# Splitting 1092 product columns at 512 and 1024 instead of 364 and 728 in an fp32r matmul kernel

## The chip, the cores and the metric

One core of a Trainium2 chip runs the kernel. The metric is the device time of one execution in microseconds (us), lower is better. Before the change it is 508.02 us, the median of two runs (507.74 and 508.31).

## The reference

A batch of 64 matrices x of 64 x 1024 is mixed along its 64 channels with weights that depend on a condition, then goes through a feed-forward layer with a low-rank branch whose rank is chosen row by row, and is added to x.

```python
# condition: two small gelu layers, softmax over K = 8 kernels
att   = softmax(gelu(gelu(cond @ W0 + b0) @ W1 + b1) @ W2 + b2)      # (64, 8)
agg_w = einsum('bk,koi->boi', att, weight);  agg_b = att @ bias_k      # (64, 64, 64), (64, 64)
h     = einsum('boi,bih->boh', agg_w, x) + agg_b[:, :, None]           # (64, 64, 1024)
# feed-forward: W is 1024 x 1024, A is 64 x 1024, gate_w is 4 x 1024
scores = h @ gate_w.T + gate_b                                         # 4 ranks: 8, 16, 32, 64
sel    = argmax(scores)                                                # top-1, its weight is 1
out    = x + h @ W.T + b + (h @ A[:r].T) @ B[:, :r].T                  # r = rank selected per row
```

## The kernel before

The 64 x 64 rows of x are taken as T = 32 tiles of 128 rows (two batch elements each). The channel mixing is moved behind the big product: for each tile the kernel first computes z = x [W | A | gate], with 1024 + 64 + 4 = 1092 columns (`NCOL`), and then multiplies z from the left by the block-diagonal mixing weights `bd`. The last 68 columns are u, from which the rank is selected and the low-rank branch computed.

Every fp32 operand is split into a high and a low part (`xth`, `xtl`; `wh`, `wl`; `zh`, `zl`; `bd` with two parts), both of type fp32r, and a product is made of three passes: high x high, low x high, high x low. The contraction of z runs over 1024 inputs in `KC` = 8 chunks k of 128. So z takes 8 x 3 matmuls for each group of columns; the stationary operand is a 128x128 block of `xth` or `xtl`, another one for each matmul, and the moving operand is a row of columns of `wh` or `wl`.

The 1092 columns are cut into `BANKS` = 3 groups of `CB` = 364 (cut by `bank_columns`, L239), each into a PSUM bank of 512 fp32. Group 2 (columns 728 to 1091) holds 296 columns of W and the 68 of u. A tile works on its groups in the `ORDER` (2, 0, 1); m is the place in that order. z of a group goes to one of two PSUM banks `p_z` in turn (`ring`); the mixed result goes to `p_out`, three banks for each of two tiles.

What each engine does for tile j, in its program's order (the kernel is written by hand with semaphores; PE executes in program order):
- PE (`step` L716, `main` L629, `mix` L640, `lora` L664): m = 0: 24 matmuls, after k = 3 `mix(j-1, 2)`, after k = 5 `lora(j-1)`; m = 1: 24 matmuls, after k = 3 `mix(j, 0)`; m = 2: 24 matmuls, after k = 3 `mix(j, 1)`, after k = 4 the transpose of u (L662). A mix is 3 matmuls (L653, L654, L657) and waits for `zl` of its group (L645). lora is 2 matmuls (L670, L671) for each of the three groups: 296 columns in group 2, 364 in the others.
- ACT: `z_hi` (L385) copies z to `zh` when the last pass of the group is done; also `xth` (L370), `bd` (L377), the transposed u (L393). In tile 1 it also copies the column sums (L436).
- DVE: `z_lo` (L480) makes `zl` = z - `zh`; then `xtl` (L457), the mixing weights (L463, L466), `residual` (L490, L493: the sum of `p_out` and `xin` into `ysum`, which shares memory with `wraw`), `route` (L514 to L535: the choice of the rank).
- POOL makes the bias terms (L322 to L337). SP issues all loads and stores.

So `mix(j-1, 2)`, which stands behind the first 12 matmuls of tile j, needs z_hi and z_lo of the group that was finished as the last of tile j-1. Tile 0 is written apart (L685 to L712): it loops over k outside and the three groups inside, as W arrives. The last tile ends with `lora` per group, `mix` (L759 to L763), `last_residual` (L496) and three stores.

Of the kernel before, what the change touches and what calls it, by code (L numbers as in the profile page):

```python
# [5 lines left out]
F32 = mybir.dt.float32  # L6
F32R = mybir.dt.float32r
ALU = mybir.AluOpType
# [24 lines left out]
def adaln_ffn(nc, x, xt, layer0, layer12, b2, kernels, bias_k, wag, b, bt, gate_b, out):  # L33
# [10 lines left out]
    RE = R + E  # L44
    NCOL = O + RE
    BANKS = 3
    CB = NCOL // BANKS
    UNROLL = 4
    ROW_BH, ROW_BL = 64, 96
    FIRST = 2  # L50
    ORDER = (2, 0, 1)
    assert P == 2 * C and HID == P and NB == C and UNROLL % 2 == 0
    assert layer0.shape[1] == NB + HID + 1 and layer12.shape[1] == HID + K + 1 and wag.shape[1] == NCOL
    assert NCOL % (2 * BANKS) == 0 and CB <= BANK and O > (BANKS - 1) * CB
    assert len(RANKS) == E and RANKS[-1] == R == C and T % UNROLL == 0 and T * K <= BANK // 2 and 2 * T <= P

    x_t = x.rearrange("(t b) c h -> t (b c) h", b=2)
# [2 lines left out]
    with ExitStack() as ctx:  # L60
# [14 lines left out]
        wl = sb("wl", [P, KC, NCOL], F32R)  # L75
        bt_h = sb("bt_h", [P, O], F32R)
        bt_l = sb("bt_l", [P, O], F32R)
        zh = sb("zh", [P, 2, CB], F32R)
        zl = sb("zl", [P, 2, CB], F32R)
        ident = sb("ident", [P, P])  # L80

        wsum = sb("wsum", [P, NCOL])
# [146 lines left out]
        def z_place(i, j, m):  # L229

            if not follows(i, j, 1) and m > 0:
                return p_out[:, 1, m - 1, 0:CB]
            return p_z[:, ring(j, m), 0:CB]

        def u_place(i, j):

# [1 line left out]

        def bank_columns(n):  # L239

            return slice(n * CB, min((n + 1) * CB, O))

        @block.sync
        def _(sp):
            sp.dma_start(cw0[:, :], layer0).then_inc(s_cond0_in, 16)
            sp.dma_start(xtin[:, 0, 0:FIRST * P], xt[0][:, 0:FIRST * P]).then_inc(s_xt_first_in, 16)
            for k in range(KC):
                sp.dma_start(wraw[:, k, :], wag[k * P:(k + 1) * P, :]).then_inc(s_w_in[k], 16)
                if k == 0:
                    sp.dma_start(xtin[:, 0, FIRST * P:], xt[0][:, FIRST * P:]).then_inc(s_xt_in[0], 16)  # L250
                    sp.dma_start(b2r[:, :], b2.partition_broadcast(NB)).then_inc(s_cond2_in, 16)
                    sp.dma_start(bk[:, :], bias_k).then_inc(s_bk_in, 16)
            sp.dma_start(xtin[:, 1, :], xt[1]).then_inc(s_xt_in[1], 16)
            for h in (slice(0, C), slice(C, P)):
                sp.dma_start(kern[h, :, :], kernels).then_inc(s_kern_in, 16)
            sp.wait_ge(s_clear, 2)
            sp.dma_start(gbias[:, R:RE], gate_b.partition_broadcast(P)).then_inc(s_gate_in, 16)
            for r in (ROW_BH, ROW_BL):
                sp.dma_start(brow[r:r + 1, :], b.rearrange("(a o) -> a o", a=1)).then_inc(s_lora_in, 16)
            for h in (slice(0, R), slice(R, P)):  # L260
                sp.dma_start(bt_raw[h, :], bt).then_inc(s_lora_in, 16)
            sp.dma_start(xin[:, 0, :], x_t[0]).then_inc(s_x_in[0], 16)
            for t in range(1, UNROLL):
                if t >= 2:
                    sp.dma_start(xtin[:, t, :], xt[t]).then_inc(s_xt_in[t], 16)
                sp.dma_start(xin[:, t, :], x_t[t]).then_inc(s_x_in[t], 16)

            def store(i, j):
                sp.wait_ge(s_y, i * UNROLL + (j + 1))
                sp.dma_start(out_t[i * UNROLL + j], ysum[:, j % 2, :]).then_inc(s_stored[j % 2], 16)  # L270

            with sp.Fori(0, T // UNROLL - 1) as i:
                for j in range(UNROLL):
                    sp.wait_ge(s_xtl, i * UNROLL + (j + 1))
                    sp.dma_start(xtin[:, j, :], xt[i * UNROLL + (j + UNROLL)]).then_inc(s_xt_in[j], 16)
                    store(i, j)
                    sp.dma_start(xin[:, j, :], x_t[i * UNROLL + (j + UNROLL)]).then_inc(s_x_in[j], 16)
            for j in range(UNROLL - 1):
                store(T // UNROLL - 1, j)
            for m, n in enumerate(ORDER):  # L280
                cols = bank_columns(n)
                sp.wait_ge(s_y, T + m)
                sp.dma_start(out_t[T - 1][:, cols], ysum[:, (T - 1) % 2, cols]).then_inc(s_stored[(T - 1) % 2], 16)
            sp.wait_ge(s_stored[0], 16 * T // 2)
            sp.wait_ge(s_stored[1], 16 * (T // 2 + BANKS - 1))

        @block.gpsimd
        def _(pool):
# [67 lines left out]
        def _(act):  # L356
# [23 lines left out]
            def z_hi(i, j, m):  # L380

                act.wait_ge(s_z, banks_before(i, j, m + 1))
                if follows(i, j, 1) or m >= 2:
                    act.wait_ge(s_mix, banks_before(i, j, m - 1))
                nc.scalar.activation(zh[:, ring(j, m), :], z_place(i, j, m), ACT.Copy).then_inc(s_zh, 1)  # L385

            def u_transposed(i, j):

# [37 lines left out]
            def step(i, j):  # L426
                if follows(i, j, 2):
                    z_hi(i, j - 1, 2)
                    if precedes(i, j):
                        xt_hi(i, j + 1)  # L430
                        bd_hi(i, j + 1)
                z_hi(i, j, 0)
                if not follows(i, j, 2):

                    act.wait_ge(s_colsum_mm, 1)
                    nc.scalar.activation(colsum[:, :].rearrange("p (a n) -> p a n", n=CB), p_out[:, 1, :, 0:CB],  # L436
                                         ACT.Copy).then_inc(s_colsum, 1)
                    bd_hi(i, j + 1)
                z_hi(i, j, 1)
                if not follows(i, j, 2):  # L440
                    u_transposed(i, j - 1)
                u_transposed(i, j)
# [5 lines left out]
        def _(dve):  # L448
# [27 lines left out]
            def z_lo(i, j, m):  # L476

                dve.wait_ge(s_zh, banks_before(i, j, m + 1))
                at = ring(j, m)
                nc.vector.tensor_tensor(zl[:, at, :], z_place(i, j, m), zh[:, at, :].bitcast(F32),  # L480
                                        ALU.subtract).then_inc(s_zl, 1)

            def residual(i, j):
# [2 lines left out]
                dve.wait_ge(s_xb, i * UNROLL + (j + 1))  # L486
                if follows(i, j, 2):
                    dve.wait_ge(s_stored[j % 2], i * 16 * (UNROLL // 2) + 16 * (j // 2))
                full = (BANKS - 1) * CB
                nc.vector.tensor_tensor(ysum[:, j % 2, 0:full].rearrange("p (a n) -> p a n", n=CB),  # L490
                                        p_out[:, j % 2, 0:BANKS - 1, 0:CB],
                                        xin[:, j % UNROLL, 0:full].rearrange("p (a n) -> p a n", n=CB), ALU.add)
                nc.vector.tensor_tensor(ysum[:, j % 2, full:O], p_out[:, j % 2, BANKS - 1, 0:O - full],  # L493
                                        xin[:, j % UNROLL, full:O], ALU.add).then_inc(s_y, 1)

            def last_residual():  # L496

                q, slot = (T - 1) % 2, (T - 1) % UNROLL
                dve.wait_ge(s_stored[q], 16 * (T // 2 - 1))
                dve.wait_ge(s_xb, T)  # L500
                for m, n in enumerate(ORDER):
                    cols = bank_columns(n)
                    dve.wait_ge(s_lora, T + m)
                    if m == BANKS - 1:
                        dve.wait_ge(s_mix, T * BANKS)
                    nc.vector.tensor_tensor(ysum[:, q, cols], p_out[:, q, n, 0:cols.stop - cols.start],
                                            xin[:, slot, cols], ALU.add).then_inc(s_y, 1)
# [1 line left out]
            def route(i, j):  # L509
# [1 line left out]
                done = i * CHAIN * UNROLL + CHAIN * j  # L511
                dve.wait_ge(s_ubias, i * UNROLL + (j + 1))
                dve.wait_ge(s_mix, banks_before(i, j, 1))
                nc.vector.tensor_tensor(u[:, :], p_out[:, j % 2, BANKS - 1, CB - RE:CB], ubias[:, j % 2, :],  # L514
                                        ALU.add).then_inc(s_chain, 1)
                dve.wait_ge(s_chain, done + 1)
                for e in range(1, E):
# [108 lines left out]
        def _(pe):  # L626
            PASSES = ((xth, wh), (xtl, wh), (xth, wl))

            def main(i, j, m, k, passes=range(3)):  # L629

                n, q = ORDER[m], j % 2
                for p in passes:
                    a, w = PASSES[p]
                    last = nc.tensor.matmul(z_place(i, j, m), a[:, q, k * P:(k + 1) * P],  # L634
                                            w[:, k, n * CB:(n + 1) * CB],
                                            start=k == 0 and p == 0, stop=k == KC - 1 and p == 2)
                if k == KC - 1 and passes[-1] == 2:
                    last.then_inc(s_z, 1)
# [1 line left out]
            def mix(i, j, m, opens=True):  # L640
# [7 lines left out]
                if m == 0:  # L648
                    pe.wait_ge(s_bdl, i * UNROLL + (j + 1))
                    if follows(i, j, 2):  # L650
                        pe.wait_ge(s_y, i * UNROLL + (j - 1))
                o = p_out[:, q, ORDER[m], 0:CB]
                nc.tensor.matmul(o, bd[:, q, 0, :], zh[:, at, :], start=opens, stop=False, skip_group_check=not opens)  # L653
                nc.tensor.matmul(o, bd[:, q, 1, :], zh[:, at, :], start=False, stop=False, skip_group_check=not opens)  # L654
                if not opens:
                    pe.wait_ge(s_zl, banks_before(i, j, m + 1))
                nc.tensor.matmul(o, bd[:, q, 0, :], zl[:, at, :], start=False, stop=True,  # L657
                                 skip_group_check=not opens).then_inc(s_mix, 1)

            def transpose_u(i, j):  # L660
                pe.wait_ge(s_um, i * UNROLL + (j + 1))
                nc.tensor.transpose(u_place(i, j), usplit[:, :], ident[:, :]).then_inc(s_ut, 1)  # L662

            def lora(i, j, bank_range=ORDER, opens=False):  # L664

                pe.wait_ge(s_utc, i * UNROLL + (j + 1))
                for n in bank_range:
# [48 lines left out]
            def step(i, j):  # L716
                first = not follows(i, j, 2)
                pe.wait_ge(s_xtl, i * UNROLL + (j + 1))
                for m in range(BANKS):
# [4 lines left out]
                    for k in range(KC):  # L724
# [3 lines left out]
                        if first and m == 1 and k == 3:  # L728
# [1 line left out]
                            pe.wait_ge(s_clear, 5)  # L730
                            pe.wait_ge(s_wsum_lo, 1)
                            for n in range(BANKS):
                                cols = slice(n * CB, (n + 1) * CB)
                                o = p_out[:, 1, n, 0:CB]
                                nc.tensor.matmul(o, ones_r[:, :], wsum_h[:, cols], start=True, stop=False)
                                last = nc.tensor.matmul(o, ones_r[:, :], wsum_l[:, cols], start=False, stop=True)
                            last.then_inc(s_colsum_mm, 1)
# [18 lines left out]
                            transpose_u(i, j)  # L756

            run(pe, step, 2)
            lora(0, T - 1, ORDER[0:1])  # L759
            lora(0, T - 1, ORDER[1:2])  # L760

            lora(0, T - 1, ORDER[2:3], opens=True)
# [36 lines left out]
```

## Time and profile before

| what | us |
|---|---|
| median of two runs | 508.02 |
| span of the profiled execution | 505.8 |
| PE busy | 478.2 (95%) |
| PE weight loads busy | 472.5 (93%) |
| DVE busy | 272.7 (54%) |
| POOL busy | 190.9 (38%) |
| ACT busy | 125.3 (25%) |

PE is TensorE's matmul side, PEld its weight-load side; both overlap, and the durations of consecutive matmuls overlap too, so that the step from one start to the next, not the mean duration, is what a matmul costs. The page's line PEclk is the granted clock of TensorE in tenths of full speed (2.4 GHz).

### The profile page before, as it was taken

The page shows a single profiled execution, that of the slowest core. Times are in us where ns is not written, and L with a number is a line of the kernel's source. Part 1 is how long each engine was busy: PE and PEld are TensorE (multiplying, and loading weights), DVE is VectorE, ACT ScalarE, POOL GpSimd, SP SyncE. Part 2 cuts the span into 40 slices and gives each one's busy share as a digit, 9 for nine tenths or more (in the row PEclk, how much of TensorE's full clock was granted, in tenths as well). Part 3 has the DMA queues.
Part 4 walks back from the last instruction along what each step waited for, and adds up shares of the span by engine and source line. Part 5 has one row for each costly group of instructions (what it writes and reads, how often), then busy time and mean ns, then how long its engine had stood idle before and what let it go on. Part 6 is the DMA issues. An engine that isn't in the chain of part 4 may idle for free.

```text
span 505.8 us, 8213 instructions
## 1 busy us (share of the span) xinstructions
PE 478.2 (95%) x2837; PEld 472.5 (93%) x2837; DVE 272.7 (54%) x665; ACT 125.3 (25%) x275; POOL 190.9 (38%) x149
## 2 busy tenths in 40 slices
PE   5578689999999999999999999999999999999996
PEld 4567589999999999999999999999999999999996
DVE  4999985445455544454555445445554454455523
ACT  6415112222212222222122222221222212122211
POOL 4994953333332233333322333332223333322200
PEclk9799799999999999999999999999999999999999
DMA  8940052233333223333322233333222333321002
GB/s 291 351 162 1 1 180 97 101 126 125 124 124 110 74 68 121 124 124 124 124 90 78 80 124 124 124 124 124 77 83 88 124 124 124 124 83 41 29 14 84
DMA packets 16270, 55.91 MB, mean 111 GB/s; under 512 B 2050, under 2 KB 2818, under 8 KB 16260
## 3 DMA queue, kind: packets, MB, share of 16 engines
q1 hardware_dynamic: 16116, 55.71, 31.2%
q8 instruction: 6, 0.10, 0.1%
q10 hardware_dynamic: 144, 0.07, 0.1%
q14 instruction: 4, 0.03, 0.0%
HBM read 39.00 MB, written 16.78 MB: 110 GB/s over the span
## 4 chain that ended last, share of the span: by engine, by line
PE 87%; DVE 9%; issue 1%; DMA 1%; ACT 1%; SPq 0%; POOL 0%; DVEq 0%; ACTq 0%; POOLq 0%
PE p_z L634 70%; PE p_out L653 3%; PE p_out L657 3%; PE p_out L654 3%; PE p_out L671 3%; PE p_out L670 3%; DVE wl L451 1%; DVE prod L463 1%; DVE xtl L457 1%; DMA b2r<-in_b 1%; DVE um L526 1%; PE p_out L634 1%; DVE bd L472 1%; PE p_z L662 1%; DVE xtl L558 1%
## 5 line engine op out<-in xcount | busy, mean ns | idle before, releaser
L634 PE MATMUL p_z<-wh,xth 128*128 128x364 f32 x752 | 251.5, 334 | 3.5 <-ACT wh L363 2.0
L634 PE MATMUL p_z<-wl,xth 128*128 128x364 f32 x752 | 248.0, 330 | 3.9 <-DVE wl L451 3.9
L634 PE MATMUL p_z<-wh,xtl 128*128 128x364 f32 x752 | 248.2, 330 | 0.0
L480 DVE TENSOR_TENSOR zl<-p_z,zh 128x364 fp32r<-128x364 f32 x94 | 50.4, 536 | 198.5 <-ACT zh L385 198.5
L634 PEld LDWEIGHTS p_z<-wh,xth 128*128 128x128 f32 x752 | 142.1, 189 | 5.8 <-ACT wh L363 2.2
L634 PEld LDWEIGHTS p_z<-wl,xth 128*128 128x128 f32 x752 | 141.9, 189 | 4.4 <-DVE wl L451 4.4
L634 PEld LDWEIGHTS p_z<-wh,xtl 128*128 128x128 f32 x752 | 142.4, 189 | 0.0
L327 POOL TENSOR_TENSOR ubias<-wsum,gbias 128x68 f32<-128x68 f32 x32 | 10.7, 333 | 256.8 <-DVE usplit L535 256.5
L385 ACT ACTIVATE zh<-p_z 128x364 fp32r<-128x364 f32 x94 | 44.7, 475 | 188.1 <-PE p_z L634 188.0
L337 POOL TENSOR_TENSOR xin<-xin,wsum 128x1024 f32<-128x1024 f32 x32 | 77.6, 2426 | 3.7 <-POOL wsum L332 2.3
L332 POOL TENSOR_TENSOR wsum<-colsum,aggb 128x1024 f32<-128x1024 f32 x32 | 60.7, 1898 | 0.7
L457 DVE TENSOR_TENSOR xtl<-xtin,xth 128x1024 fp32r<-128x1024 f32 x31 | 41.1, 1327 | 15.3 <-ACT xth L370 15.3
L653 PE MATMUL p_out<-zh,bd 128*128 128x364 f32 x96 | 32.2, 336 | 9.5 <-DVE zl L480 7.1
L370 ACT ACTIVATE xth<-xtin 128x1024 fp32r<-128x1024 f32 x31 | 32.9, 1060 | 1.4 <-DMA xtin<-in_xt 0.7
L657 PE MATMUL p_out<-zl,bd 128*128 128x364 f32 x96 | 31.7, 331 | 0.0
L654 PE MATMUL p_out<-zh,bd 128*128 128x364 f32 x96 | 31.7, 330 | 0.0
L393 ACT ACTIVATE ut_hl<-p_z 128x128 fp32r<-128x128 f32 x32 | 8.9, 278 | 91.5 <-PE p_z L662 91.5
L671 PE MATMUL p_out<-bt_l,ut_h 128*128 128x364 f32 (+1 forms) x96 | 31.0, 323 | 0.0
L670 PE MATMUL p_out<-bt_h,ut_hl 128*128 128x364 f32 (+1 forms) x96 | 30.3, 324 | 0.0
L377 ACT ACTIVATE bd<-aggw 64x64 fp32r<-64x64 f32 x32 | 8.2, 256 | 84.9 <-DVE aggw L466 84.9
L653 PEld LDWEIGHTS p_out<-zh,bd 128*128 128x128 f32 x96 | 18.1, 189 | 10.7 <-DVE zl L480 6.2
L490 DVE TENSOR_TENSOR wraw<-p_out,xin 128x728 f32<-128x728 f32 x31 | 28.1, 905 | 0.0
(92 smaller groups left out, 373.0 us busy)
## 6 DMA issues: line engine op xcount, KB each, us to landing
xin<-in_x SPq DMA_DIRECT2D x32, 512.0 KB, 4.5
xtin<-in_xt SPq DMA_DIRECT2D x31, 512.0 KB, 5.0
out<-wraw SPq DMA_DIRECT2D x31, 512.0 KB, 3.0
wraw<-in_wag SPq DMA_DIRECT2D x8, 546.0 KB, 7.5
bt_raw<-in_bt SPq DMA_DIRECT2D x2, 256.0 KB
xtin<-in_xt SPq DMA_DIRECT2D x1, 384.0 KB, 5.3
out<-wraw SPq DMA_DIRECT2D x2, 182.0 KB, 2.2
kern<-in_kernels SPq DMA_DIRECT2D x2, 128.0 KB, 11.1
```

The source lines that it names most:

```text
L332: nc.gpsimd.tensor_tensor(bias[:, 0:O], colsum[:, 0:O], aggb[:, t, :].broadcast_to([P, O]), ALU.mult).then_inc(s_bias_x, 1)
L337: nc.gpsimd.tensor_tensor(xs, xs, bias[:, 0:O], ALU.add).then_inc(s_xb, 1)
L370: nc.scalar.activation(xth[:, j % 2, :], xtin[:, j % UNROLL, :], ACT.Copy).then_inc(s_xth, 1)
L385: nc.scalar.activation(zh[:, ring(j, m), :], z_place(i, j, m), ACT.Copy).then_inc(s_zh, 1)
L457: nc.vector.tensor_tensor(xtl[:, j % 2, :], xtin[:, j % UNROLL, :], xth[:, j % 2, :].bitcast(F32), ALU.subtract).then_inc(s_xtl, 1)
L480: nc.vector.tensor_tensor(zl[:, at, :], z_place(i, j, m), zh[:, at, :].bitcast(F32), ALU.subtract).then_inc(s_zl, 1)
L634: last = nc.tensor.matmul(z_place(i, j, m), a[:, q, k * P:(k + 1) * P], w[:, k, n * CB:(n + 1) * CB], start=k == 0 and p == 0, stop=k == K ...
L653: nc.tensor.matmul(o, bd[:, q, 0, :], zh[:, at, :], start=opens, stop=False, skip_group_check=not opens)
L654: nc.tensor.matmul(o, bd[:, q, 1, :], zh[:, at, :], start=False, stop=False, skip_group_check=not opens)
L657: nc.tensor.matmul(o, bd[:, q, 0, :], zl[:, at, :], start=False, stop=True, skip_group_check=not opens).then_inc(s_mix, 1)
L670: nc.tensor.matmul(o, ut_hl[:, :], bt_h[:, cols], start=opens, stop=False, skip_group_check=True)
L671: last = nc.tensor.matmul(o, ut_h1[:, :], bt_l[:, cols], start=False, stop=True, skip_group_check=True)
```

## The change

The groups become columns 0 to 511, 512 to 1023 and 1024 to 1091: two full banks and the 68 columns of u alone. The number of matmuls of `main` and `mix` stays at three groups per k and pass; of each three, one now has 68 columns and two have 512. lora, which has no part in u, goes over two groups of 512 in place of three (296, 364, 364). The residual is one DVE instruction of 1024 columns in place of two (728 and 296). The column sums are copied by two ACT instructions (1024 and 68) in place of one. The last tile has two residual steps and two stores in place of three. `ORDER` stays (2, 0, 1), so the group of u is the first of each tile.

```diff
-    CB = NCOL // BANKS
+    COLS = ((0, BANK), (BANK, O), (O, NCOL))
...
         def bank_columns(n):
-            return slice(n * CB, min((n + 1) * CB, O))
+            return slice(*COLS[n])
+
+        def width(n):
+            return COLS[n][1] - COLS[n][0]
...
-            for m, n in enumerate(ORDER):
+            for m, n in enumerate(ORDER[1:]):
                 cols = bank_columns(n)
                 sp.wait_ge(s_y, T + m)
                 sp.dma_start(out_t[T - 1][:, cols], ysum[:, (T - 1) % 2, cols]).then_inc(s_stored[(T - 1) % 2], 16)
...
-                nc.scalar.activation(zh[:, ring(j, m), :], z_place(i, j, m), ACT.Copy).then_inc(s_zh, 1)
+                nc.scalar.activation(zh[:, ring(j, m), 0:width(ORDER[m])], z_place(i, j, m), ACT.Copy).then_inc(s_zh, 1)
...
-                    nc.scalar.activation(colsum[:, :].rearrange("p (a n) -> p a n", n=CB), p_out[:, 1, :, 0:CB],
-                                         ACT.Copy).then_inc(s_colsum, 1)
+                    nc.scalar.activation(colsum[:, 0:O].rearrange("p (a n) -> p a n", n=BANK), p_out[:, 1, 0:2, :], ACT.Copy)
+                    nc.scalar.activation(colsum[:, O:NCOL], p_out[:, 1, 2, 0:RE], ACT.Copy).then_inc(s_colsum, 1)
...
-                nc.vector.tensor_tensor(zl[:, at, :], z_place(i, j, m), zh[:, at, :].bitcast(F32),
+                n = width(ORDER[m])
+                nc.vector.tensor_tensor(zl[:, at, 0:n], z_place(i, j, m), zh[:, at, 0:n].bitcast(F32),
                                         ALU.subtract).then_inc(s_zl, 1)
...
-                full = (BANKS - 1) * CB
-                nc.vector.tensor_tensor(ysum[:, j % 2, 0:full] ...
-                nc.vector.tensor_tensor(ysum[:, j % 2, full:O], p_out[:, j % 2, BANKS - 1, 0:O - full],
-                                        xin[:, j % UNROLL, full:O], ALU.add).then_inc(s_y, 1)
+                nc.vector.tensor_tensor(ysum[:, j % 2, :].rearrange("p (a n) -> p a n", n=BANK),
+                                        p_out[:, j % 2, 0:BANKS - 1, :],
+                                        xin[:, j % UNROLL, :].rearrange("p (a n) -> p a n", n=BANK),
+                                        ALU.add).then_inc(s_y, 1)
...
-                nc.vector.tensor_tensor(u[:, :], p_out[:, j % 2, BANKS - 1, CB - RE:CB], ubias[:, j % 2, :],
+                nc.vector.tensor_tensor(u[:, :], p_out[:, j % 2, BANKS - 1, 0:RE], ubias[:, j % 2, :],
...
                     last = nc.tensor.matmul(z_place(i, j, m), a[:, q, k * P:(k + 1) * P],
-                                            w[:, k, n * CB:(n + 1) * CB],
+                                            w[:, k, bank_columns(n)],
...
-                o = p_out[:, q, ORDER[m], 0:CB]
-                nc.tensor.matmul(o, bd[:, q, 0, :], zh[:, at, :], start=opens, ...)
+                n = width(ORDER[m])
+                o = p_out[:, q, ORDER[m], 0:n]
+                nc.tensor.matmul(o, bd[:, q, 0, :], zh[:, at, 0:n], start=opens, ...)
...
-            def lora(i, j, bank_range=ORDER, opens=False):
+            def lora(i, j, bank_range=ORDER[1:], opens=False):
...
             run(pe, step, 2)
-            lora(0, T - 1, ORDER[0:1])
             lora(0, T - 1, ORDER[1:2])
```

## Rows read from the trace of the kernel before

**Rows 1.** The page: span, PE and PE weight loads, granted clock in 40 slices.
```profile
span 505.8 us, 8213 instructions
...
PE 478.2 (95%) x2837; PEld 472.5 (93%) x2837; DVE 272.7 (54%) x665; ACT 125.3 (25%) x275; POOL 190.9 (38%) x149
...
PEclk9799799999999999999999999999999999999999
```

**Rows 2.** Waits in total: who waited for whom, us, times, longest.
```profile
PE p_out L653 <- DVE zl L480: 7.1, 3, 5.2
```

**Rows 3.** The chain that ended last, from tile 30 on: start, us, what.
```profile
484.01 0.11 PE p_z L662
...
489.09 0.14 PE p_out L670
...
489.36 0.17 PE p_out L670
...
493.54 4.00 PE p_z L634 x24
...
498.53 0.11 PE p_z L662
```

**Rows 4.** Timeline of PE, tile 0: start, us, engine, line, what.
```profile
19.98 0.51 PE L634 MATMUL p_out<-wh,xth 128*128 128x364 f32 x1
...
20.89 0.51 PE L634 MATMUL p_out<-wh,xtl 128*128 128x364 f32 x1
```

**Rows 5.** Timeline of tile 2, where PE waited for DVE: weight loads and matmuls.
```profile
71.04 0.54 DVE L480 TENSOR_TENSOR zl<-p_z,zh 128x364 fp32r<-128x364 f32 x1 [1.08 <-ACT zh L385]
...
71.70 0.19 PEld L653 LDWEIGHTS p_out<-zh,bd 128*128 128x128 f32 x1 [1.82 <-issue]
71.71 0.43 PE L653 MATMUL p_out<-zh,bd 128*128 128x364 f32 x1 [1.52 <-DVE zl L480]
71.81 0.19 PEld L654 LDWEIGHTS p_out<-zh,bd 128*128 128x128 f32 x1
...
71.98 0.19 PEld L657 LDWEIGHTS p_out<-zl,bd 128*128 128x128 f32 x1
```

**Rows 6.** Timeline of PE weight loads around the transpose of a steady tile.
```profile
251.53 0.19 PEld L634 LDWEIGHTS p_z<-wh,xth 128*128 128x128 f32 x1
251.64 0.19 PEld L634 LDWEIGHTS p_z<-wh,xtl 128*128 128x128 f32 x1
```

**Rows 7.** Timeline across the boundary of two steady tiles.
```profile
252.97 0.33 PE L634 MATMUL p_z<-wl,xth 128*128 128x364 f32 x1
...
253.33 0.48 ACT L385 ACTIVATE zh<-p_z 128x364 fp32r<-128x364 f32 x1 [0.98 <-PE p_z L634]
...
253.84 0.54 DVE L480 TENSOR_TENSOR zl<-p_z,zh 128x364 fp32r<-128x364 f32 x1 [4.07 <-ACT zh L385]
...
254.92 1.23 DVE L457 TENSOR_TENSOR xtl<-xtin,xth 128x1024 fp32r<-128x1024 f32 x1 [0.55 <-ACT xth L370]
...
255.11 0.33 PE L653 MATMUL p_out<-zh,bd 128*128 128x364 f32 x1
...
257.77 0.25 ACT L378 ACTIVATE bd<-aggw 64x64 fp32r<-64x64 f32 x1
```

**Rows 8.** The page's groups: copies on ACT and DVE of two widths.
```profile
L480 DVE TENSOR_TENSOR zl<-p_z,zh 128x364 fp32r<-128x364 f32 x94 | 50.4, 536 | 198.5 <-ACT zh L385 198.5
...
L385 ACT ACTIVATE zh<-p_z 128x364 fp32r<-128x364 f32 x94 | 44.7, 475 | 188.1 <-PE p_z L634 188.0
...
L393 ACT ACTIVATE ut_hl<-p_z 128x128 fp32r<-128x128 f32 x32 | 8.9, 278 | 91.5 <-PE p_z L662 91.5
```

**Rows 9.** One line of the trace: the addition that makes u, 68 columns.
```profile
L514 DVE TENSOR_TENSOR u<-p_out,ubias x32: 213/228/229, 47.9 to 493.6; 128x68 f32<-128x68 f32 x32
```

**Rows 10.** The chain in tile 0: start, us, what.
```profile
26.07 0.60 PE p_out L709 x4
...
27.22 1.95 DVE wl L451
```

More of the change, by code:

```diff
@@ L53, in adaln_ffn @@
     assert layer0.shape[1] == NB + HID + 1 and layer12.shape[1] == HID + K + 1 and wag.shape[1] == NCOL
-    assert NCOL % (2 * BANKS) == 0 and CB <= BANK and O > (BANKS - 1) * CB
+    assert O == 2 * BANK and RE <= BANK - P and RE % 2 == 0
     assert len(RANKS) == E and RANKS[-1] == R == C and T % UNROLL == 0 and T * K <= BANK // 2 and 2 * T <= P
@@ L77, in adaln_ffn @@
         bt_l = sb("bt_l", [P, O], F32R)
-        zh = sb("zh", [P, 2, CB], F32R)
-        zl = sb("zl", [P, 2, CB], F32R)
+        zh = sb("zh", [P, 2, BANK], F32R)
+        zl = sb("zl", [P, 2, BANK], F32R)
         ident = sb("ident", [P, P])
@@ L231, in z_place @@
             if not follows(i, j, 1) and m > 0:
-                return p_out[:, 1, m - 1, 0:CB]
-            return p_z[:, ring(j, m), 0:CB]
+                return p_out[:, 1, m - 1, 0:width(ORDER[m])]
+            return p_z[:, ring(j, m), 0:width(ORDER[m])]
         def u_place(i, j):
@@ L284, in _ @@
             sp.wait_ge(s_stored[0], 16 * T // 2)
-            sp.wait_ge(s_stored[1], 16 * (T // 2 + BANKS - 1))
+            sp.wait_ge(s_stored[1], 16 * (T // 2 + BANKS - 2))
         @block.gpsimd
@@ L488, in residual @@
                     dve.wait_ge(s_stored[j % 2], i * 16 * (UNROLL // 2) + 16 * (j // 2))
-                full = (BANKS - 1) * CB
-                nc.vector.tensor_tensor(ysum[:, j % 2, 0:full].rearrange("p (a n) -> p a n", n=CB),
-                                        p_out[:, j % 2, 0:BANKS - 1, 0:CB],
-                                        xin[:, j % UNROLL, 0:full].rearrange("p (a n) -> p a n", n=CB), ALU.add)
-                nc.vector.tensor_tensor(ysum[:, j % 2, full:O], p_out[:, j % 2, BANKS - 1, 0:O - full],
-                                        xin[:, j % UNROLL, full:O], ALU.add).then_inc(s_y, 1)
+                nc.vector.tensor_tensor(ysum[:, j % 2, :].rearrange("p (a n) -> p a n", n=BANK),
+                                        p_out[:, j % 2, 0:BANKS - 1, :],
+                                        xin[:, j % UNROLL, :].rearrange("p (a n) -> p a n", n=BANK),
+                                        ALU.add).then_inc(s_y, 1)
             def last_residual():
@@ L500, in last_residual @@
                 dve.wait_ge(s_xb, T)
-                for m, n in enumerate(ORDER):
+                for m, n in enumerate(ORDER[1:]):
                     cols = bank_columns(n)
                     dve.wait_ge(s_lora, T + m)
-                    if m == BANKS - 1:
+                    if m == BANKS - 2:
                         dve.wait_ge(s_mix, T * BANKS)
@@ L651, in mix @@
                         pe.wait_ge(s_y, i * UNROLL + (j - 1))
-                o = p_out[:, q, ORDER[m], 0:CB]
-                nc.tensor.matmul(o, bd[:, q, 0, :], zh[:, at, :], start=opens, stop=False, skip_group_check=not opens)
-                nc.tensor.matmul(o, bd[:, q, 1, :], zh[:, at, :], start=False, stop=False, skip_group_check=not opens)
+                n = width(ORDER[m])
+                o = p_out[:, q, ORDER[m], 0:n]
+                nc.tensor.matmul(o, bd[:, q, 0, :], zh[:, at, 0:n], start=opens, stop=False, skip_group_check=not opens)
+                nc.tensor.matmul(o, bd[:, q, 1, :], zh[:, at, 0:n], start=False, stop=False, skip_group_check=not opens)
                 if not opens:
                     pe.wait_ge(s_zl, banks_before(i, j, m + 1))
-                nc.tensor.matmul(o, bd[:, q, 0, :], zl[:, at, :], start=False, stop=True,
+                nc.tensor.matmul(o, bd[:, q, 0, :], zl[:, at, 0:n], start=False, stop=True,
                                  skip_group_check=not opens).then_inc(s_mix, 1)
@@ L732, in step @@
                             for n in range(BANKS):
-                                cols = slice(n * CB, (n + 1) * CB)
-                                o = p_out[:, 1, n, 0:CB]
+                                cols = bank_columns(n)
+                                o = p_out[:, 1, n, 0:width(n)]
                                 nc.tensor.matmul(o, ones_r[:, :], wsum_h[:, cols], start=True, stop=False)
```

## The prediction

> **What bounds the kernel now.** I read the page first: PE is busy 95% of the span at the full granted clock but for a few early slices [rows 1]. The waits come next: the longest entry in which PE waits for another engine's data is 7.1 us in three waits, all before 72 us [rows 2, 5]. Then the chain of what ended last: from 71.7 us to the end it is PE alone, tile after tile. From transpose to transpose a tile takes 498.53 - 484.01 = 14.52 us [rows 3]; the other periods I read between 72 and 492 us are 14.51. Last I read PE's timeline for starts: a duration of 0.33 us overlaps its neighbour, so a matmul costs the step to the next one. So what a change is worth is a sum of steps on PE, per tile, plus any wait that PE newly has.
>
> **The price of a matmul by its columns.** 24 matmuls of 364 columns take 4.00 us, 0.166 us each; the two of 296 columns take 489.36 - 489.09 = 0.27 us, 0.135 each [rows 3]. In tile 0, at half clock (1.2 GHz), three steps of 364 columns take 20.89 - 19.98 = 0.91 us, 0.303 each [rows 4], which is one column per cycle (364 / 1.2 = 303 ns). At 2.4 GHz that stream is 152 ns and of 296 columns 123 ns, so 0.012 to 0.014 us stay per matmul, whatever its width. 512 columns then stream for 213 ns and cost 0.213 + 0.0145 = 0.228 us. The upper bound is a price that is all per column: 0.166 / 364 x 512 = 0.234; the lower bound takes the 0.012 of the narrower row: 0.225. By this price alone nothing changes: 27 x (0.028 + 0.0145) + 58 x 0.228 is 14.4 us, since the columns are the same.
>
> **But 68 columns stream for 28 ns, and each matmul has a weight load of its own.** The load of the next block runs under the present matmul, and starts when that matmul takes its own weights. Where PE starts from a stand, that load is not covered, and it can be read: the load starts at 71.70, the next load at 71.81, when the first matmul has its weights (its record of 0.43 us in place of 0.33 says the same: 0.10 of waiting for weights), and from there on the step is 0.166 again [rows 5]. Behind the transpose, whose matmul has only 128 columns, two loads start 0.11 us apart [rows 6]. So a load holds the way for 0.11 us. Under 364 columns it is hidden; under 68 it is not, and 12 or more such matmuls stand one behind the other, so nothing evens it out. I take 0.11 us for each narrow matmul. Lower bound 0.043 us (28 ns and the fixed part, loads fully hidden). Upper bound 0.189 us, the whole duration of a load record [rows 5, 6]; against it speaks that the records of 0.19 already overlap their successors at steps of 0.11 and 0.166.
>
> A page of the Trainium skill speaks for the cheap end: "TensorE: Matmul & The Clock Gate", section "Back-to-back issue gap", gives N/2.4 + 2.5 ns for an isolated matmul, 31 ns at 68 columns. By it the 27 narrow matmuls of a tile would cost 0.8 us in place of 3.0. Its figure for 364 columns would be 154 ns, where the rows have 166, so the rows decide.
>
> **A tile, part by part.** Per tile there are 24 + 3 narrow matmuls (main and mix of u's group), 48 + 6 wide ones, and lora's 4 wide ones in place of 6.
> - wide: 58 x 0.228 = 13.22
> - narrow: 27 x 0.11 = 2.97
> - the transpose: 0.11 as before [rows 3]
> - sum 16.30, which is 1.79 above 14.51.
>
> **A wait that is new.** `mix(j-1, 2)` stands behind the first 12 matmuls of a tile and needs zh and zl of the group finished last. Count from the start of that group's last matmul, T = 252.97. Now: zh starts at T + 0.36, zl at T + 0.87 and ends at T + 1.41; the mix comes at T + 2.14 [rows 7], so 0.7 us are to spare. After: z is done 0.06 later (213 - 152 ns), zh starts at T + 0.42. ACT's copies of 364 and 128 columns take 475 and 278 ns [rows 8], 0.835 ns per column, so 512 take 0.598: zl starts 0.51 + 0.12 later, T + 1.05. DVE takes 536 ns for 364 columns [rows 8] and 228 for 68 [rows 9], 1.04 ns per column, so 512 take 0.69: T + 1.74. From the end of zl (71.04 + 0.54) to the moment the waiting matmul has its weights (71.81) are 0.23 us [rows 5]: T + 1.97. PE itself is there at T + 0.228 + 12 x 0.11 = T + 1.55, since u's group is first and now short. The wait costs 0.42 us per tile. Zero, if the chain is faster than I say, and 0.6 are its ends. The sum is now 16.72, 2.21 above 14.51.
>
> What stands behind this wait on PE is everything, so it is paid in full. The other waits keep their cover. `mix(j, 1)` has 12 wide matmuls (2.7 us) between its product and itself, against the same chain of 1.97. zl of u's group stands behind xtl, the mixing weights and the copies of bd. From the start of xtl to the end of these copies are 257.77 + 0.25 - 254.92 = 3.10 us [rows 7]; xtl now starts near T + 2.1, so with 0.23 each for zh and zl of 68 columns they end near T + 5.7, wanted at T + 4.9 + 2.7 = 7.6. The residual is one instruction less and DVE is 54% busy [rows 1]; stores and loads follow a slower PE.
>
> **Start and end.** In tile 0 the chain passes through PE until the four small matmuls at 26.07, which DVE waits for before its next wl at 27.22 [rows 10]. Up to there k = 2 to 4 lie on the path, one at half clock: 6 x 0.427 + 3 x 0.22 against 9 x 0.303 is +0.5, and twice 6 x 0.228 + 3 x 0.11 against 9 x 0.166 is +0.4; together +0.9. From there to 71.7 DVE sets the pace: PE waited 5.2 us for zl in tile 1 [rows 2] and 1.5 in tile 2 [rows 5], so what PE's tiles 1 and 2 add up to the mix at 71.7 lies under these waits, as do the column sums' copy in two parts (about +0.2) and what tile 0 adds after k = 4. If the cover were gone it would be 2 to 3 us. At the end the chain from z over zh and zl to the last residual is longer by 0.34 (above), 0.06 for a wide third matmul and 0.15 for 512 columns on DVE: +0.6 with the store, which is larger and one fewer.
>
> **Sum.** From the mix of tile 2 at 71.7 to the end of the last product are 29 periods and the rest of tile 2 (39 wide for 364, 3 narrow: +2.2), so 30 x 2.21 = 66.3. With 0.9 and 0.6 it is 67.8: the span goes from 505.8 to 573.6. The median stands 2.2 us above the span (508.02), so I predict 575.8, say **576 us**, a ratio of 1.134.
>
> **Rivals.**
> - *Loads don't bind* (narrow at 0.043). Then PE reaches the mix at T + 0.75 and waits 1.22 there: 13.22 + 1.16 + 0.11 + 1.22 = 15.71, +1.20 x 30 and 1 for start and end: 545 us. Against it rows 5 and 6. By the page cited above it would be near this as well, since the chain over ACT and DVE then sets the boundary. Chance 0.09.
> - *A load costs its whole record*, 0.189. PE reaches the mix at T + 2.5, without a wait: 13.22 + 5.10 + 0.11 = 18.43, +3.9 x 30: 627 us. Chance 0.08, with narrow prices from 0.14 up.
> - *The clock falls.* A narrow stretch has the array streaming a quarter of the time. The clock was at half for the matmuls behind the 5.2 us wait in tile 1, and full behind the wait of 1.5 us [rows 2, 5]; the narrow stretch is 1.3 us with a wait of 0.4, then wide ones come. If each tile ran its first group at half clock it would lose about 4 us: 690 us. Chance 0.04.
> - *The columns alone decide: no change.* This is the other side: the whole chain at the boundary has to fit under 12 matmuls of 0.043, 0.75 us behind T; it decides against a loss only from there down. It is 1.41 now, before it gets longer [rows 7]. It would give 14.4 per tile, 508 us or a trifle less (lora's two matmuls fewer save 0.03 us per tile). Chance 0.03; faster by over 2% 0.01 of it.
>
> **How the numbers follow.** The forecast has 0.76. Its own range: wide 0.225 to 0.234 gives -5 to +11 us, narrow 0.10 to 0.125 gives -8 to +12, both partly taken back by the wait (a slower narrow matmul arrives later, 12 of 27), the wait -13 to +5: 560 to 594. To hold the time 8 times in 10 it reaches down to the first rival: 546 to 596. A difference of about 2% is what a measurement of this kernel can tell from no change; slower by more holds 0.97, within 0.02, faster 0.01.
>
> **What would show it.** In the profile after: steps of 0.228 between wide matmuls, of 0.11 between narrow ones with loads 0.11 apart; a wait of PE at L653's line for zl in about 30 tiles, 0.3 to 0.5 us each; a period of 16.7 us; the granted clock still full; ACT copies of 0.60 and DVE ones of 0.69. It is wrong if the narrow steps are below 0.08 or above 0.14, or if the boundary shows no wait.

## The result, and the profile after

The changed kernel takes 584.31 us (median of two runs, 582.57 to 586.05) against 508.02 before: ratio 1.149, 95% interval 1.146 to 1.153. It is slower by 15%.

The page of the changed kernel; beside [rows 1] it is the span and the weight loads' share that moved (93% to 79%), while PE's share is the same 95%:

```profile
span 584.5 us, 8053 instructions
...
PE 554.9 (95%) x2773; PEld 461.4 (79%) x2773; DVE 271.3 (46%) x633; ACT 125.4 (21%) x276; POOL 191.0 (33%) x149
...
PEclk9989789999999999999999999999999999999999
```

Its waits in total, PE's matmul and load side (who, for whom, us, times, longest), the answer to [rows 2]. Three waits have become one in each tile:

```profile
PEld p_out L657 <- DVE zl L485: 16.9, 32, 4.4
...
PE p_out L657 <- DVE zl L485: 10.4, 31, 4.0
```

Its chain of what ended last; the same place of two tiles in a row (start, us, what). A period is 264.68 - 247.75 = 16.93 us, where before it was 14.52 [rows 3]. Every fourth period is 17.01 us, as between the last two lines; over 28 tiles the mean is 16.95:

```profile
247.75 5.66 PE p_z L637 x24
...
264.68 5.66 PE p_z L637 x24
...
281.69 5.66 PE p_z L637 x24
```

Its timeline across the boundary of two steady tiles, all engines, the answer to [rows 6] and [rows 7] (start, us, engine, line, what, idle time before):

```profile
256.61 0.39 PE L637 MATMUL p_z<-wl,xth 128*128 128x512 f32 x1
...
256.84 0.19 PE L637 MATMUL p_z<-wh,xth 128*128 128x68 f32 x1
256.85 0.19 PEld L637 LDWEIGHTS p_z<-wh,xtl 128*128 128x128 f32 x1
...
256.95 0.19 PEld L637 LDWEIGHTS p_z<-wl,xth 128*128 128x128 f32 x1
256.98 0.28 PE L637 MATMUL p_z<-wl,xth 128*128 128x68 f32 x1
257.04 0.60 ACT L389 ACTIVATE zh<-p_z 128x512 fp32r<-128x512 f32 x1 [1.66 <-PE p_z L637]
...
257.68 0.69 DVE L485 TENSOR_TENSOR zl<-p_z,zh 128x512 fp32r<-128x512 f32 x1 [5.68 <-ACT zh L389]
...
257.96 0.19 PEld L637 LDWEIGHTS p_z<-wl,xth 128*128 128x128 f32 x1
257.99 0.28 PE L637 MATMUL p_z<-wl,xth 128*128 128x68 f32 x1
258.42 0.19 PEld L657 LDWEIGHTS p_out<-zh,bd 128*128 128x128 f32 x1 [0.27 <-DVE zl L485]
258.42 0.50 PE L657 MATMUL p_out<-zh,bd 128*128 128x512 f32 x1 [0.15 <-DVE zl L485]
258.53 0.19 PEld L658 LDWEIGHTS p_out<-zh,bd 128*128 128x128 f32 x1
```

Read it from the loads. From 256.85 to 257.96 there are ten steps between loads, 0.111 us each, although 68 columns would stream in 28 ns at one column per cycle (an estimate from [rows 4]): that the array goes at the pace of its weights is the reading that two runs below put to the test. The next load would start at 258.07. It starts at 258.42, 0.05 after DVE has finished zl (257.68 + 0.69): a wait of 0.35 us. In the tiles of the longer periods ACT's copy starts 0.08 later and the wait is 0.43. After it a matmul of 512 columns again covers its successor's load.

### The profile page after: what moved, and what is told of

Same layout as the page of the kernel before. It is cut to its first block, busy times and chain, and to the rows that moved or that the text cites. A ratio compares the mean times of both kernels' runs of the same rounds, so it can differ in the third digit from the quotient of the medians.

```text
span 584.5 us, 8053 instructions
## 1 busy us (share of the span) xinstructions
PE 554.9 (95%) x2773; PEld 461.4 (79%) x2773; DVE 271.3 (46%) x633; ACT 125.4 (21%) x276; POOL 191.0 (33%) x149
## 4 chain that ended last, share of the span: by engine, by line
PE 84%; DVE 10%; ACT 3%; issue 1%; DMA 1%; SPq 0%; POOL 0%; ACTq 0%; POOLq 0%; DVEq 0%
PE p_z L637 66%; PE p_out L657 4%; DVE zl L485 4%; PE p_out L661 3%; PE p_out L658 3%; ACT zh L389 3%; PE p_out L674 3%; PE p_out L675 2%; DVE wl L455 1%; PE p_out L637 1%; DMA b2r<-in_b 1%; DVE um L529 1%; PE p_z L666 1%; DVE xtl L461 1%; DVE xtl L561 1%
## 5 line engine op out<-in xcount | busy, mean ns | idle before, releaser
L637 PE MATMUL p_z<-wh,xth 128*128 128x68 f32 (+1 forms) x752 | 268.5, 357 | 5.0 <-ACT wh L367 2.8
L637 PE MATMUL p_z<-wl,xth 128*128 128x68 f32 (+1 forms) x752 | 267.7, 357 | 3.2 <-DVE wl L455 3.2
L637 PE MATMUL p_z<-wh,xtl 128*128 128x68 f32 (+1 forms) x752 | 268.4, 357 | 0.0
L485 DVE TENSOR_TENSOR zl<-p_z,zh 128x512 fp32r<-128x512 f32 (+1 forms) x94 | 50.2, 534 | 251.8 <-ACT zh L389 251.8
L389 ACT ACTIVATE zh<-p_z 128x512 fp32r<-128x512 f32 (+1 forms) x94 | 44.5, 473 | 234.6 <-PE p_z L637 233.9
L657 PE MATMUL p_out<-zh,bd 128*128 128x512 f32 (+1 forms) x96 | 35.9, 374 | 13.0 <-DVE zl L485 10.4
L494 DVE TENSOR_TENSOR wraw<-p_out,xin 128x1024 f32<-128x1024 f32 x31 | 37.8, 1220 | 0.4
L661 PE MATMUL p_out<-zl,bd 128*128 128x512 f32 (+1 forms) x96 | 35.2, 367 | 0.0
L658 PE MATMUL p_out<-zh,bd 128*128 128x512 f32 (+1 forms) x96 | 34.8, 363 | 0.0
L674 PE MATMUL p_out<-bt_h,ut_hl 128*128 128x512 f32 x64 | 28.2, 440 | 0.0
L467 DVE TENSOR_TENSOR prod<-kern,attp 128x512 f32<-128x512 f32 x32 | 26.4, 825 | 0.0
```

The costliest lines, as they stand in the source:

```text
L389: nc.scalar.activation(zh[:, ring(j, m), 0:width(ORDER[m])], z_place(i, j, m), ACT.Copy).then_inc(s_zh, 1)
L485: nc.vector.tensor_tensor(zl[:, at, 0:n], z_place(i, j, m), zh[:, at, 0:n].bitcast(F32), ALU.subtract).then_inc(s_zl, 1)
L494: nc.vector.tensor_tensor(ysum[:, j % 2, :].rearrange("p (a n) -> p a n", n=BANK), p_out[:, j % 2, 0:BANKS - 1, :], xin[:, j % UNROLL, :]. ...
L657: nc.tensor.matmul(o, bd[:, q, 0, :], zh[:, at, 0:n], start=opens, stop=False, skip_group_check=not opens)
L658: nc.tensor.matmul(o, bd[:, q, 1, :], zh[:, at, 0:n], start=False, stop=False, skip_group_check=not opens)
L661: nc.tensor.matmul(o, bd[:, q, 0, :], zl[:, at, 0:n], start=False, stop=True, skip_group_check=not opens).then_inc(s_mix, 1)
```

## The experiments

There are eight. later_mix, half_weights, u_236 and split_428 ran beside one another on one chip, the other four on another, each set with the kernel before (507.61 us on the first chip, 508.08 on the second); each ratio is to the kernel before on the same chip.

**The changed kernel once more.**

> The changed kernel once more, beside the others on the same chip: 584 us, with half clock again in the first tiles if that belongs to the kernel and not to the one execution profiled.

Measured: 584.19 us, ratio 1.148 (1.144 to 1.152); span 582.4, the steady period again 16.93 us. Half clock was there again in the first tiles (below). In what follows this run is the measure for experiments on the changed kernel, three of which ran on the other chip, where the kernel before is 0.5 us faster. Its four executions lie between 580.7 and 584.6 us.

**The wait: the mix six matmuls later.**

```diff
-                        if not first and m == 0 and k == 3:
+                        if not first and m == 0 and k == 5:
                             mix(i, j - 1, 2)
```

> The changed kernel with one edit: mix(j-1, 2) stands behind 18 matmuls of a steady tile instead of 12 (ahead of lora(j-1), which already stood there). Theory (the chain over zh and zl makes PE wait about 0.45 us in each of 30 tiles): PE gets to the mix 6 x 0.11 = 0.67 us later than before, so the wait goes: 584.3 - 30 x 0.45, about 571 us, and no wait of PE at the mix in steady tiles. Rival (the wait only takes the place of the weights' loads or of work that comes later, and the matmuls alone set the time): no change, 584 us.

Measured: 571.8 us, ratio 1.126 (1.124 to 1.128). Its timeline shows the mix right behind the 18th narrow matmul, at the step of 0.11, with no idle time:

```profile
252.07 0.28 PE L637 MATMUL p_z<-wh,xtl 128*128 128x68 f32 x1
252.18 0.28 PE L637 MATMUL p_z<-wl,xth 128*128 128x68 f32 x1
252.29 0.48 PE L657 MATMUL p_out<-zh,bd 128*128 128x512 f32 x1
```

and its chain, the same place of two tiles, a period of 16.60 us in place of 16.93:

```profile
224.67 5.66 PE p_z L637 x24
241.27 5.66 PE p_z L637 x24
```

So the wait was real and on the path. All periods are now 16.60, and against the mean of 16.95 that is 0.35 us for each of 30 tiles, 10.5 of the 12 us. It was a little shorter than the 0.42 of the prediction. The other 64 us over the kernel before are not the wait.

**The narrow matmul: its loads or its issue?**

```diff
-                    last = nc.tensor.matmul(z_place(i, j, m), a[:, q, k * P:(k + 1) * P],
+                    half = m == 0 and follows(i, j, 2)
+                    place = z_place(i, j, m)
+                    last = nc.tensor.matmul(place[0:C, :] if half else place, a[:, q, k * P:k * P + (C if half else P)],
```

> The changed kernel, but in steady tiles the 24 narrow matmuls of the main product load only 64 of 128 weight columns, so that rows 64 to 127 of u are not computed (old values stay there). All 68 columns still stream. Theory (the weight load sets the narrow step): a load of half the columns takes half the time, the step falls from 0.112 to about 0.056 us. The wait at the mix then grows by 12 x 0.056 = 0.67 to about 1.1 us, as the chain over zh and zl is the same: per tile 24 x 0.056 - 0.67 = 0.67 us are saved, 564 us. Rival (a floor of 0.11 us for each matmul instruction, in its issue, whatever it loads): the step stays 0.11 and the time 584 us.

Measured: 567.7 us, ratio 1.118 (1.116 to 1.121). Loads of 64 columns (C = 64) in a steady tile, and the mix behind the twelfth:

```profile
265.95 0.14 PEld L639 LDWEIGHTS p_z<-wl,xth 128*64 128x64 f32 x1
266.01 0.14 PEld L639 LDWEIGHTS p_z<-wh,xth 128*64 128x64 f32 x1
266.07 0.14 PEld L639 LDWEIGHTS p_z<-wh,xtl 128*64 128x64 f32 x1
```

```profile
267.20 0.50 PE L659 MATMUL p_out<-zh,bd 128*128 128x512 f32 x1 [0.82 <-DVE zl L485]
```

The step is 0.058 us where it was 0.111, with as many instructions and as many streamed columns. The step follows the columns of weights: the load is what a narrow matmul costs, and an issue floor of 0.11 us does not exist. (Half the weight columns are also half the rows of the result; that writing the result is not the limit is shown by the next run, which writes 3.5 times the columns into all 128 rows at the same step.) The trace agrees with the Trainium skill here ("TensorE: Matmul & The Clock Gate", section "LDWEIGHTS (loading the stationary operand)"): P/1.2 ns for P weight columns, 107 and 53 ns, where 111 and 58 are measured. The wait at the mix grew to about 1 us; of 24 x 0.053 = 1.27 us per tile only 0.53 came out as a shorter period (16.42 us against 16.95): 0.64 went into the longer wait, as the chain over zh and zl kept its length, and two of the narrow steps stay at 0.11, since the load behind them is again one of 128 columns. With its narrow loads halved, the kernel is still 60 us slower than the one before.

**The narrow matmul: its columns.**

```diff
-    COLS = ((0, BANK), (BANK, O), (O, NCOL))
+    UW = 236
+    COLS = ((0, BANK), (BANK, O), (NCOL - UW, NCOL))
```

(the copies of u and of its column sums read the last 68 of these columns)

> The changed kernel, but u's group takes 236 columns (856 to 1091) instead of 68; 168 of them are computed a second time and not used. Theory (a matmul costs the larger of its weight load, 0.11 us, and 0.456 ns per column): 236 columns stream for 0.108 us, so the narrow steps stay at 0.11 and the time stays at 584 us within 3. Rival (a fixed part and a price per column, nothing else): each narrow matmul costs 168 x 0.42 = 0.07 us more, 27 per tile, less what the wait at the mix gives back (0.45 at most): 1.45 us per tile, about 628 us.

Measured: 581.6 us, ratio 1.146 (1.143 to 1.149). 168 columns more in each of 27 matmuls per tile, and the time does not rise (the interval overlaps that of the changed kernel, 1.144 to 1.152). Steady narrow steps, 0.11 us:

```profile
252.62 0.27 PE L638 MATMUL p_z<-wh,xth 128*128 128x236 f32 x1
252.73 0.28 PE L638 MATMUL p_z<-wh,xtl 128*128 128x236 f32 x1
252.84 0.27 PE L638 MATMUL p_z<-wl,xth 128*128 128x236 f32 x1
```

> The changed kernel, but u's group takes 300 columns (792 to 1091), 232 of them a second time and unused. Theory (the larger of load and stream): 300 columns cost 0.137 us, 0.025 more than 68 for each of 27 narrow matmuls, less 12 x 0.025 = 0.3 that the wait at the mix gives back: +0.38 us per tile, about 595 us. The clock should stay full in the first tiles, where the changed kernel shows it at half, if it is the array's idle time in the narrow stretches that lowers it. Rival (fixed part and price per column): +0.096 us each, +2.2 us per tile, 650 us.

Measured: 593.9 us, ratio 1.169 (1.166 to 1.172); 595 was expected with the larger of load and stream, 650 with a fixed part added. The steady narrow step is now 0.137:

```profile
260.49 0.30 PE L638 MATMUL p_z<-wh,xth 128*128 128x300 f32 x1
260.62 0.30 PE L638 MATMUL p_z<-wh,xtl 128*128 128x300 f32 x1
260.76 0.30 PE L638 MATMUL p_z<-wl,xth 128*128 128x300 f32 x1
```

The two widths bracket the point where the stream becomes the longer one.

The same two runs bear on another question. In the changed kernel the granted clock falls to half in tile 2, behind the wait for tile 1's last group; with 236 and with 300 columns it does not. First the changed kernel once more, then u_236; columns: stretch, its length, busy us (x instructions) of PE, PEld, DVE, ACT, POOL, then the granted clock, DMA share, GB/s:

```profile
65.00:70.00 5.00, 3.54 (x15) 3.04 (x15) 5.00 (x4) 0.69 (x1) 4.89 (x3) 0.75 0.60 199
70.00:75.00 5.00, 5.00 (x17) 4.17 (x16) 3.47 (x6) 0.74 (x3) 1.06 (x2) 0.57 0.34 122
```

```profile
65.00:70.00 5.00, 3.75 (x25) 3.25 (x24) 5.00 (x4) 0.90 (x1) 4.84 (x4) 1.00 0.58 204
70.00:75.00 5.00, 4.39 (x22) 3.31 (x21) 3.94 (x7) 0.88 (x3) 1.16 (x2) 1.00 0.32 117
```

From their timelines, first the changed kernel once more, then u_236: the mix of tile 1's last group and the mix of tile 2's first, between which this stretch lies:

```profile
66.70 0.50 PE L657 MATMUL p_out<-zh,bd 128*128 128x512 f32 x1 [1.46 <-DVE zl L485]
...
75.72 0.19 PE L657 MATMUL p_out<-zh,bd 128*128 128x68 f32 x1
```

```profile
66.78 0.50 PE L658 MATMUL p_out<-zh,bd 128*128 128x512 f32 x1 [1.25 <-DVE zl L486]
...
73.40 0.37 PE L658 MATMUL p_out<-zh,bd 128*128 128x236 f32 x1 [0.61 <-DVE zl L486]
```

9.02 us against 6.62: in this execution the half clock costs 2.4 us once. The profiled spans differ by 1.9 us (582.4 and 580.5), so it is most likely why the run with more work isn't the slower one; but the medians, 2.6 us apart, were taken on two chips, and their ratios to the kernel before can't be told apart. Nor is it shown that the width of the narrow matmuls is what brings the clock down. All four profiles with 68 columns have the half clock in tile 2 (both of the changed kernel, later_mix, half_weights), behind waits of 0.7 to 2.0 us, and u_236 and u_300 don't, behind 1.25 and 0.73. But in split_428_later_mix below it falls in tile 2 with 236 columns.

**Unequal groups without a narrow one.** The kernel before with other cuts; group 2 gets what is left:

```diff
-    CB = NCOL // BANKS
+    CB = 428
+    LAST = NCOL - 2 * CB
```

> The kernel before with the groups cut at 428 and 856, so that the last has 236 columns (168 of W and the 68 of u); the work is that of before. Theory: wide matmuls cost 428 x 0.456 = 0.195 us, those of 236 columns 0.112 (the load), the third lora group of 168 columns as much: 54 x 0.195 + 27 x 0.112 + 4 x 0.195 + 2 x 0.112 + 0.11 = 14.7 us per tile, and a wait of 0.25 at the mix behind the first 12 matmuls: 14.9, against 14.51 before: about 520 us. Rival (unequal groups cost by the width of the widest, or by a clock that falls in narrow stretches): 540 us or more. Second rival (the columns alone decide): 508 us.

Measured: 518.6 us, ratio 1.023 (1.021 to 1.026), 520 expected. Its chain has a period of 235.52 - 220.69 = 14.83 us:

```profile
220.69 4.68 PE p_z L641 x24
235.52 4.68 PE p_z L641 x24
```

> The kernel before with the groups cut at 428 and 856 and mix(j-1, 2) behind 18 matmuls of a tile instead of 12. Theory: the wait at the mix (0.25 us per tile, if it is there at 428) goes, and what is left over the kernel before are the loads that 236 columns do not quite cover: 14.7 us per tile, about 513 us. Rival (no wait was there at 428): the same time as without the move.

Measured: 513.9 us, ratio 1.011 (1.009 to 1.013); the period is 14.65 us. So at 428 too, part of the loss was the wait (0.18 us per tile, 0.25 expected). The other part, 0.13 us per tile, is roughly what the loads that narrow matmuls don't cover come to; by an estimate from the steps measured here they are 27 x (0.111 - 236 x 0.000455) = 0.10 for the 236 columns and 2 x (0.111 - 168 x 0.000455) = 0.07 for lora's group of 168. The profile of this run also has the granted clock at half for about 3 us in tile 2 (steps of 0.36 from 73.30 to 76.47, 0.195 otherwise), behind a wait of 1.8 us, which costs it 1.5 us once:

```profile
72.28 0.37 PE L661 MATMUL p_out<-zh,bd 128*128 128x236 f32 x1 [1.82 <-DVE zl L487]
...
73.98 0.56 PE L641 MATMUL p_z<-wl,xth 128*128 128x428 f32 x1
74.33 0.56 PE L641 MATMUL p_z<-wh,xth 128*128 128x428 f32 x1
```

> The kernel before with the groups cut at 400 and 800; the last has 292 columns, above the width at which stream and load are equal (0.112 / 0.456 ns = 245 columns). Theory: all matmuls of main and mix cost 0.456 ns per column, as before; lora's third group of 224 columns costs 0.112 instead of 0.102. A tile is 14.55 us against 14.51, and PE reaches the mix at T + 1.81, after the chain's 1.72: no wait. About 509 us. Rival (any unequal split costs): 515 us or more.

Measured: 507.0 us, ratio 0.998 (0.997 to 0.999). Above the load's length the cut is free: 24 matmuls of 400 columns take 4.36 to 4.38 us, 0.182 each, and the period is 14.50 us or 14.48 in turn, 14.49 in the mean, against 14.52:

```profile
217.37 4.38 PE p_z L641 x24
231.87 4.36 PE p_z L641 x24
```

That is the 1 us by which this run is ahead (30 x 0.03). No cut that was tried beats three equal groups by more than that; the place of the narrow group within the tile was not varied.

## Why the prediction was right, and where it was off

576 us were predicted with a range of 546 to 596; 584.3 were measured. Both mechanisms were there, and both at their place. One step failed, the cover at the start, and two terms were mis-sized in opposite directions (the wide matmul too cheap, the wait too long), so that the sum per tile came out 0.22 us short.

- *Loads of narrow matmuls lie open*: 0.11 us predicted from the load behind a wait [rows 5] and the one behind the transpose [rows 6]; 0.111 measured in steady tiles, and half_weights and u_236 show that it is the load and not the issue or the columns. The rival with hidden loads falls. The isolated gap of the Trainium skill that the prediction weighs ("TensorE: Matmul & The Clock Gate", section "Back-to-back issue gap": 31 ns at 68 columns, against 111 here) was no evidence for it: the same section says that at small N this formula under-counts, because it leaves no room for the weight load. The rival with the load's whole record (0.189) falls too.
- *A new wait at the mix*: 0.42 predicted, 0.35 measured, and 0.43 in every fourth tile; later_mix takes it away. The copies have the predicted lengths: 0.60 for 512 columns on ACT, 0.69 on DVE. The term that was too long is the way from the end of zl to the waiting matmul's load: 0.12 before [rows 5], 0.05 in steady tiles after.
- *The wide matmul* is the term of the steady sum that was mis-sized. I took 0.228 from a fixed 0.0145 us above one column per cycle; 24 matmuls of 512 columns behind a covered load take 5.58 us in u_236, 0.2325 each, near the upper bound of 0.234 that I had set. 58 x 0.0045 is 0.26 us per tile, 8 us in 30 tiles. Between 364 and 512 columns the price grows by 0.066 us, 0.445 ns per column, so most of what stands above one column per cycle grows with the width. The rows of 296 and 364 columns lie too near each other to tell a fixed part from one that grows.
- Together: 58 x 0.2325 + 27 x 0.111 + 0.11 + 0.34 = 16.93 us, which is the measured period; predicted were 16.72. With the mean of 16.95 against 14.52 it makes 30 x 2.43 = 72.9 of the 76.6 us between the spans of before and of the changed kernel's second profile (after_again); with 4.0 at the start and -0.2 at the end (below) the sum is 76.7.
- *The start* was put at +0.9 us. The mix of tile 2 comes at 75.72 in that second profile and at 71.71 before: +4.0. The step that failed is the sentence that from 26 us on DVE sets the pace up to there and hides what PE adds. The first +0.9 is right: DVE's wl starts at 28.14 where it started at 27.22 [rows 10]. But the column sums, which the prediction puts under the cover, are not under it:

```profile
44.59 0.41 PE L735 MATMUL p_out<-wsum_h,ones_r 128*128 128x364 f32 x1 [1.46 <-DVE wsum_l L594]
...
64.51 0.44 PE L653 MATMUL p_out<-zh,bd 128*128 128x364 f32 x1 [0.32 <-DVE zl L480]
```

```profile
46.34 0.40 PE L739 MATMUL p_out<-wsum_h,ones_r 128*128 128x512 f32 x1
```

  Before (first), PE waits for DVE there; in the second profile after, DVE has finished wsum_l at 45.11 (42.64 + 2.47) and PE comes only at 46.34, with the granted clock at half from 37 to 44 us, where before it was full (in u_300, where it was full there too, PE waits for DVE again, 0.37 us). The column sums pass over ACT and POOL into u of tile 0 on DVE, which starts at 49.73 in place of 47.93, and the mix of tile 1's last group at 66.70 in place of 64.51: +2.2. Then the clock fell once more, and at half clock PE, not DVE, set the arrival at tile 2's mix. In u_236, which also has the first half clock but not the second, that mix comes at 73.40, +1.7, with PE waiting for DVE again. So the cover gave way by 0.8 us at the column sums and by 2.3 in tile 2. "The clock falls" stood among the rivals as something of each tile, at 690 us; it came in the first tiles alone. The price that the prediction names for a lost cover, 2 to 3 us, is about what it cost.
- *The end* was put at +0.6 and is the same as before: from the start of the last matmul of the main product (499.80 and 578.65) to the end of the span are 6.0 us before and 5.8 after (first profile of the changed kernel; 5.8 in the second as well). That one store fewer and a residual in two parts made up for the longer copies is likely, but wasn't tried.
- The median of before stood 2.2 us above the span of its profile, and the prediction carried that over. After, it stands 0.2 us below, because the slower of the two executions was the one profiled (586.05 us, span 584.5). Each timed execution is 1.5 to 1.9 us longer than its own span; the rest is the difference between one execution and another, which a sum from a profile can't give.
- Of the 8.5 us by which 575.8 is short, 0.22 x 30 = 6.6 are steady tiles and 3.1 the start, and about 1.1 came back from the end (0.8) and from the step from span to median (0.3). The wait, 0.07 per tile too long, hid a part of what the wide matmul is too cheap; that is luck, but a small one.

That nothing changes because the columns are the same (the rival on the other side) fails twice: at the load, and at the boundary.

## What to carry to other kernels

Where each matmul has its own weights, a matmul of fewer columns than its load takes time for (here about 245: 0.111 us at 0.455 ns per column) costs as much as one of that width (68 and 236 columns cost the same, 300 more); cut a row of columns so that each part stays above it, whether the cuts fall on full banks made no difference here (0.454 to 0.458 ns per column at 364, 400, 428 and 512). A short group at the front of a tile also shortens the time after which the results of the last group are wanted, and a longer last group makes them later: both ends of that race move together, so place the consumer by time and not by the number of matmuls ahead of it.

## What the runs showed of the hardware that was not expected

- At full clock a matmul with its own fp32r weights costs 0.166 us at 364 columns, 0.182 at 400, 0.195 at 428 and 0.2325 at 512, that is 0.454 to 0.458 ns per column, where one column per cycle at 2.4 GHz would be 0.417; at half clock it is one column per cycle (0.303 us at 364) [rows 4]. What the 9% at full clock are was not tried. The narrow step follows the clock too: 0.21 us at half clock (after_again, 67.54 to 68.39), where the load holds the way for 0.111 at full clock.
- The granted clock fell to half (1.2 GHz) in tile 2 in all four profiles with 68 columns, after waits of 0.71 (later_mix), 1.45 and 1.46 (the changed kernel) and 1.97 us (half_weights) that stood among these narrow matmuls, the mix's three of 512 columns having followed the wait. It stayed full after 1.25 us among matmuls of 236 columns (u_236) and 0.73 among those of 300 (u_300), and in the kernel before after 1.5 us among those of 364 [rows 5]; but it also fell after 1.8 us in split_428_later_mix, and not after 1.1 in split_428. In steady tiles, with the same narrow stretch and a wait of 0.35, or about 1 us in half_weights, it stayed full. What decides is open: each of these is one execution.
